# Attention scores from one stacked 128-row product and one 64-row product in two row tiles, with V's bias added later

## What is computed

```
xn   = group_norm(x, 32 groups) * w + b
qkv  = W_qkv @ xn + b_qkv              # 1536 x 512; 8 heads, 64 channels each for q, k, v
s    = (q^T k) / sqrt(64)              # per head, 1024 x 1024
p    = softmax(s over keys)
a    = p v^T                           # per head, 1024 x 64
out  = x + W_proj @ a + b_proj
```

## Time and profile before

| | |
|---|---|
| median of 3 runs | 4349.01 us (4347.39 to 4350.95) |
| span of the profiled execution | 4346.0 us |
| time around the span, to the median | 3.0 us |
| mean granted TensorE clock | 0.999 of full speed |
| busy share PE, DVE, ACT, POOL | 99, 76, 66, 58% |

### The profile page before, as it was taken

The page is one execution under the profiler, slowest core; times in us unless marked ns, Lnnn a source line. Parts: engine busy times, 40 slices in busy tenths (PEclk is TensorE's granted clock), DMA queues, the critical chain, the costliest instruction groups (busy, mean ns, idle before and its releaser), DMA issues.

```text
span 4346.0 us, 89905 instructions
## 1 busy us (share of the span) xinstructions
PE 4295.6 (99%) x26692; PEld 3736.9 (86%) x26692; DVE 3313.6 (76%) x5483; ACT 2875.3 (66%) x5317; POOL 2505.1 (58%) x2406
## 2 busy tenths in 40 slices
PE   7999999999999999999999999999999999999999
PEld 6888888888888888888888888888888888888887
DVE  5777867788687786777867778687786877868778
ACT  4757747477474775747757476574765747667476
POOL 5655556565564655656566565565655646556465
PEclk9999999999999999999999999999999999999999
DMA  3232222322223222222222222222222222223222
GB/s 87 48 96 47 71 72 48 96 47 80 64 46 96 49 78 64 56 86 49 80 71 66 81 46 80 65 66 79 48 79 64 71 71 49 79 64 82 60 49 92
DMA packets 99933, 295.61 MB, mean 68 GB/s; under 512 B 15136, under 2 KB 15264, under 8 KB 99616
## 3 DMA queue, kind: packets, MB, share of 16 engines
q1 hardware_dynamic: 99616, 291.71, 25.0%
HBM read 123.88 MB, written 33.55 MB: 36 GB/s over the span
## 4 chain that ended last, share of the span: by engine, by line
PE 95%; DVE 2%; issue 1%; POOL 1%; ACT 1%; DMA 0%; SPq 0%; DVEq 0%; ACTq 0%; POOLq 0%
PE ps_t L760 21%; PE ps_g L714 15%; PE ps_o L772 11%; PE ps_o L773 11%; PE ps_s L751 11%; PE ps_s L749 11%; PE ps_s L714 7%; PE ps_t L714 6%; PE ps_o L714 3%; POOL x_raw L389 1%; ACT probs L479 0%; DVE spread L603 0%; DVE pt_lo L569 0%; DVE work L601 0%; PE ps_t L778 0%
## 5 line engine op out<-in xcount | busy, mean ns | idle before, releaser
L383 POOL TENSOR_SCALAR probs<-probs,row_rcp 128x1024 f32<-128x1024 f32 x1024 | 1149.9, 1123 | 1375.5 <-DVE row_rcp L564 1374.0
L560 DVE TENSOR_REDUCE row_min<-ps_s 128x1 f32<-128x1024 f32 x1024 | 1250.2, 1221 | 220.5 <-PE ps_s L751 205.0
L484 ACT CAST pt_hi<-ps_t 128x512 fp32r<-128x512 f32 x2048 | 1110.6, 590 | 446.5 <-PE ps_t L760 431.7
L569 DVE TENSOR_TENSOR pt_lo<-ps_t,pt_hi 128x512 fp32r<-128x512 f32 x2048 | 1308.5, 679 | 9.5 <-ACT pt_hi L484 5.0
L479 ACT ACTIVATE probs<-ps_s,row_min 128x1024 f32<-128x1024 f32 x1024 | 1150.7, 1124 | 215.5 <-DVE row_min L560 202.5
L760 PEld LDWEIGHTS ps_t<-const_sb,probs 128*128 128x128 f32 x8192 | 944.3, 140 | 185.5 <-DVE pt_lo L569 57.0
L760 PE MATMUL ps_t<-const_sb,probs 128*128 128x128 f32 x8192 | 1085.9, 274 | 0.8
L772 PE MATMUL ps_o<-pt_hi,v_st 128*128 128x256 f32 x4096 | 1044.4, 288 | 0.0
L773 PE MATMUL ps_o<-pt_lo,v_st 128*128 128x256 f32 x4096 | 1014.8, 282 | 0.0
L751 PE MATMUL ps_s<-kl_st,q_st 128*128 128x512 f32 x2048 | 808.3, 395 | 0.0
L772 PEld LDWEIGHTS ps_o<-pt_hi,v_st 128*128 128x128 f32 x4096 | 771.6, 188 | 39.4 <-issue 12.4
(11 more groups left out here) (110 smaller groups left out, 4918.2 us busy)
## 6 DMA issues: line engine op xcount, KB each, us to landing
wqk_raw<-in_wqk SPq DMA_DIRECT2D x130, 256.0 KB, 2.7
q_st<-kh_st SPq DMA_DIRECT2D x128, 256.0 KB, 2.9
q_st<-kl_st SPq DMA_DIRECT2D x128, 256.0 KB, 3.6
kh_st<-kh_st SPq DMA_DIRECT2D x128, 256.0 KB, 2.9
kl_st<-kl_st SPq DMA_DIRECT2D x128, 256.0 KB, 3.5
x_raw<-layer_out SPq DMA_DIRECT2D x36, 512.0 KB, 5.0
wv_raw<-in_wv SPq DMA_DIRECT2D x68, 256.0 KB, 3.6
x_raw<-in_x SPq DMA_DIRECT2D x32, 512.0 KB, 5.3
```

Of the source, the lines that this page charges most:

```text
L383: nc.gpsimd.tensor_scalar(probs[m % 2][:, :], probs[m % 2][:, :], row_rcp[:, m % 4:m % 4 + 1], 1.0, ALU.mult, ALU.mult).then_inc(probs_rea ...
L484: nc.scalar.copy(pt_hi[:, m // 2 % 2, 4 * half:4 * half + 4, (m % 2) * P:(m % 2 + 1) * P], ps_t[:, half, :].rearrange("p (b t) -> p b t", ...
L560: nc.vector.tensor_reduce(row_min[:, m % 4:m % 4 + 1], ps_s[:, m % 2, :], AX.X, ALU.min).then_inc(min_ready, 1)
L569: nc.vector.tensor_tensor(pt_lo[place], ps_t[:, half, :].rearrange("p (b t) -> p b t", b=4), f32(pt_hi[place]), ALU.subtract).then_inc(lo_ ...
```

## The change

`scores` still has four matmuls of 512 columns per tile. The first two are the 128-row products of the stacked q (high over low) with the stacked high keys, one for each half of the keys. The other two contract 64 rows only, q high with k low. The one for the first 512 keys reads partitions 0 to 63 (`q_st` and `kl_st`), the one for the second 512 reads partitions 64 to 127 (a new tile `q2_st`, and `kl_st`); they write different PSUM banks. The product of the two low parts is no longer made.

`stack` gets a third copy before its inner wait (q high to the bottom of `q2_st`), and its last copy moves half as many columns.

V's bias leaves `evac_v`, which becomes a plain copy, and is added in `add_halves`, which becomes a three-operand instruction with the bias of the channel as a scalar. (The weights of a softmax row sum to one, so the bias passes through.) The broadcast `bv_all` gives way to a small `bv_sb`. The small statistics tiles become slices of one tile.

```diff
-        bv_all = sb("bv_all", [P, LAYERS, C], F32)
+        q2_st = [sb(f"q2_st{s}", [P, T], F32R) for s in range(2)]
+        bv_sb = sb("bv_sb", [P, LAYERS * KT], F32)
...
                 sp.dma_start(f32(q_st[s][0:D, :]), f32(kh_st[s][0:D, :])).then_inc(q_moved, 16)
                 sp.dma_start(f32(q_st[s][D:P, :]), f32(kl_st[s][0:D, :])).then_inc(q_moved, 16)
-                sp.wait_ge(q_moved, 32 * (hd + 1))
+                sp.dma_start(f32(q2_st[s][D:P, :]), f32(kh_st[s][0:D, :])).then_inc(q_moved, 16)
+                sp.wait_ge(q_moved, 48 * (hd + 1))
                 sp.dma_start(f32(kh_st[s][0:D, :]), f32(kh_st[s][D:P, :])).then_inc(stacked[s], 16)
-                sp.dma_start(f32(kl_st[s][0:D, :]), f32(kl_st[s][D:P, :])).then_inc(stacked[s], 16)
+                sp.dma_start(f32(kl_st[s][0:D, 0:HALF]), f32(kl_st[s][D:P, 0:HALF])).then_inc(stacked[s], 16)
...
-            sp.dma_start(bv_all[:, :, :], bv.rearrange("(o l) n -> o l n", o=1).broadcast_to([P, LAYERS, C])).then_inc(const_loaded, 16)
+            sp.dma_start(bv_sb[:, :], bv).then_inc(const_loaded, 16)
...
-                nc.vector.tensor_tensor(attn[rows, cols], ps_o[rows, 0:GROUP], o_part[k % 2][rows, :],
-                                        ALU.add).then_inc(attn_ready, 1)
+                nc.vector.scalar_tensor_tensor(out=attn[rows, cols], in0=ps_o[rows, 0:GROUP],
+                                               scalar=bv_sb[rows, bass.ds(lay * KT + p, 1)], in1=o_part[k % 2][rows, :],
+                                               op0=ALU.add, op1=ALU.add).then_inc(attn_ready, 1)
...
-                nc.vector.tensor_tensor(v_raw[:, b, :].rearrange("p (o n) -> p o n", o=1),
-                                        v_bank[b].rearrange("p (o n) -> p o n", o=1),
-                                        bv_all[:, bass.ds(lay, 1), :], ALU.add).then_inc(v_evac, 1)
+                nc.vector.tensor_copy(v_raw[:, b, :], v_bank[b]).then_inc(v_evac, 1)
...
-                j = m % NT
-                for half in range(2):
-                    cols = slice(half * HALF, (half + 1) * HALF)
-                    nc.tensor.matmul(ps_s[:, m % 2, cols], q_st[s][:, j * P:(j + 1) * P], kh_st[s][:, cols],
-                                     start=True, stop=False)
-                    mm = nc.tensor.matmul(ps_s[:, m % 2, cols], q_st[s][:, j * P:(j + 1) * P], kl_st[s][:, cols],
-                                          start=False, stop=True)
+                tile = slice((m % NT) * P, (m % NT + 1) * P)
+                top, low = slice(0, D), slice(D, P)
+                first, second = slice(0, HALF), slice(HALF, T)
+                for cols in (first, second):
+                    nc.tensor.matmul(ps_s[:, m % 2, cols], q_st[s][:, tile], kh_st[s][:, cols], start=True, stop=False)
+
+                nc.tensor.matmul(ps_s[:, m % 2, first], q_st[s][top, tile], kl_st[s][top, first], start=False, stop=True)
+                mm = nc.tensor.matmul(ps_s[:, m % 2, second], q2_st[s][low, tile], kl_st[s][low, second],
+                                      start=False, stop=True)
                 mm.then_inc(scores_ready, 1)
```

More of the change, by code:

```diff
@@ L119, in build @@
         bo_sb = sb("bo_sb", [P, LAYERS * KT], F32)
+        bv_sb = sb("bv_sb", [P, LAYERS * KT], F32)
         nw_sb = sb("nw_sb", [P, LAYERS * KT], F32)
         nb_sb = sb("nb_sb", [P, LAYERS * KT], F32)
[L122 to L125, removed]
+        row_stats = sb("row_stats", [P, 16], F32)
+        qk_scale = row_stats[:, 12:13]
+        row_min, row_sum, row_rcp = (row_stats[:, 4 * n:4 * n + 4] for n in range(3))
         bn_part = sb("bn_part", [P, KT, 12], F32)
@@ L570, in low_part, with add_halves @@
                                         f32(pt_hi[place]), ALU.subtract).then_inc(lo_ready, 1)
-            def add_halves(pair, k):
+            def add_halves(pair, lay, p, k):
                 rows = slice(0, D) if k < 4 else slice(D, P)
@@ L627, in x_low, with evac_v @@
                                         ALU.subtract).then_inc(xn_ready, 1)
-            def evac_v(i, lay, b):
+            def evac_v(i, b):
                 dve.wait_ge(v_acc, 8 * i + b + 1)
-                nc.vector.tensor_tensor(v_raw[:, b, :].rearrange("p (o n) -> p o n", o=1),
-                                        v_bank[b].rearrange("p (o n) -> p o n", o=1),
-                                        bv_all[:, bass.ds(lay, 1), :], ALU.add).then_inc(v_evac, 1)
+                nc.vector.tensor_copy(v_raw[:, b, :], v_bank[b]).then_inc(v_evac, 1)
             def output(i, lay, q):
@@ L662, in _, with pair_steps @@
                 x_low(0, c)
-            def pair_steps(i, p, last):
+            def pair_steps(i, lay, p, last):
                 pair = PAIRS * i + p
@@ L668, in pair_steps @@
                     if not last and m >= 4 and m % 2 == 0:
-                        add_halves(pair, m // 2 - 2)
+                        add_halves(pair, lay, p, m // 2 - 2)
                     if not (last and m + 2 >= PT_STEPS):
@@ L674, in pair_steps @@
                     if m == PT_STEPS - 1 or last and m >= 3 and m % 2 == 1:
-                        add_halves(pair, (m - 3) // 2)
+                        add_halves(pair, lay, p, (m - 3) // 2)
                     if not (last and m + 2 >= PT_STEPS):
@@ L685, in pair_steps @@
                     group_spread(i + 1)
-                add_halves(pair, 7)
+                add_halves(pair, lay, p, 7)
             with dve.Fori(0, PASSES) as i:
@@ L690, in _ @@
                 for b in range(4):
-                    evac_v(i, lay, b)
+                    evac_v(i, b)
                 for m in range(2):
                     smallest(TILES * i + m, m)
-                    evac_v(i, lay, 4 + 2 * m)
+                    evac_v(i, 4 + 2 * m)
                     reciprocal(TILES * i + m, m)
-                    evac_v(i, lay, 5 + 2 * m)
+                    evac_v(i, 5 + 2 * m)
                 with dve.Fori(0, PAIRS - 1) as p:
-                    pair_steps(i, p, False)
-                pair_steps(i, PAIRS - 1, True)
+                    pair_steps(i, lay, p, False)
+                pair_steps(i, lay, PAIRS - 1, True)
                 norm_coefs(i + 1, within(next_pass(i) // B, 0, LAYERS - 1))
@@ L921 @@
         "bqk": columns(qkv_b[:, :, 0:2].reshape(LAYERS, H * P)),
-        "bv": qkv_b[:, :, 2].reshape(LAYERS, C),
+        "bv": columns(qkv_b[:, :, 2].reshape(LAYERS, C)),
         "bo": columns(both("proj_b", "out_b")),
```

## The result

The changed kernel takes 4450.48 us (median of 4 runs, 4449.88 to 4450.77), the one before 4348.27 us (4 runs): a ratio of 1.0234, 95% interval 1.0219 to 1.0248. It is 102 us slower. The forecast was 4264 us and faster; the range, 4175 to 4505, holds the time, on its slow side. The rival "the passages drain the array" had forecast 4498.

A forecast was written before the change was run, and what follows sets the result against it. TensorE was taken as the bound, with DVE pacing some steps. Scores -89, bias +5 and start -1 gave -85 us against a span of 4346.0, so 4261, and 4264 us with the 3.0 around it; range 4175 to 4505.

The forecast's parts named there:

- the passages drain the array: Rival: each change between 128-row and 64-row products costs 0.16 us, one load exposed, -0.196 a tile, 4498 us; chance 0.25.
- the third price: In scores, the array's change from 128-row to 64-row products and back, twice per tile: taken as nothing, bounds 0 to 0.27 each.
- The second price: In scores, weight loads of the two 64-row matmuls: only one made ahead, so the second tile starts 0.109 us late.
- Drained, and loads only after it: Rival: each change of row count waits for the array to empty, then loads; -0.415 us a tile, 4721 us; chance 0.12.
- The first price: In scores, whether the two 64-row matmuls overlap: taken as yes, costing one matmul, 0.2325 us, and not two.
- Which tiles collect it: Tiles gaining the 0.124 us: 14 in each of three pairs, 1 in the last, 2 in the opening; 720 in all, 89 us.
- The cover that the rivals took: TensorE's waits for DVE, taken to absorb loss in the drain rivals: 0.4 us a pair, 2.3 in a pass's last pair.
- Stacking: Third copy ahead of the inner wait: a delay of 1 to 2 us in the opening, hidden; cost nothing.
- Bias: Three-operand add_halves takes 0.03 us more where DVE paces, 11 times in each of 16 passes: +5 us; evac_v nothing.
- The start: TensorE's first matmul waits until 12.10 us for bv_all; the small bias load lands 1 us earlier: -1 us.
- both loads hidden: Rival: both 64-row weight loads hidden and changes of row count free, saving 0.2325 us a tile, 4186 us; chance 0.20.
- the forecast's own sum: Scores per tile: 0.2325 saved less 0.109 for one exposed load, 0.124 us; lost from 0.062 us per change of row count.

The follow-up runs named there:

- e3: Changed kernel with both 64-row products on the same row tile (partitions 0 to 63), so not side by side: 4675.52 us, ratio 1.0756 to before.
- e1: Kernel before, its scores and stacking kept, with only V's bias moved into the addition of the halves: 4359.6 us against 4346.77, ratio 1.003.
- e8: Kernel before, with V's bias added by ACT in its copy of the other half and DVE's addition two-operand: 4383.08 us against 4353.95, ratio 1.0065.
- e2: Changed kernel with the two low products made as 128-row products; order, third copy and moved bias kept: 4361.39 us against 4346.77, ratio 1.0033.
- e5: Changed kernel with the 64-row pair ahead of the two 128-row score products: 4488.39 us against 4353.95, ratio 1.0307.
- e9: Changed kernel, timing only, with the 64-row pair made twice on even tiles and never on odd: 4320.93 us against before's 4347.16, ratio 0.9939.
- e4: Changed kernel with score matmuls ordered high, low, high, low, so four changes of row count per tile and no overlap: 5067.46 us, ratio 1.1658 to before.
- e7: Full-row version of the changed kernel with its two low products cut to 96 rows: 4367.12 us against before's 4353.95, ratio 1.0029.

## Why the prediction was wrong

**The step that failed is the third price**, "the passages at nothing, since the nearest row of a change of kind shows nothing". They cost 0.20 and 0.15 us, against bounds of 0 and 0.27. The row that I leaned on, scores to transposes without a gap, has both sides at 128 rows; it says that operands of another kind cost nothing, and can't say what other tiles cost. The Trainium skill, "TensorEngine Tiling (Array Packing)", Key Properties, has the rule that I set beside it: a change of tiling mode drains the engine. These traces agree with it in kind: no load and no matmul of the new mode starts until 0.32 us after the start of the last matmul of the old one. Here a passage costs 0.15 to 0.20 us: 0.09 of waiting, and 0.11 or, in front of the transposes, 0.06 for a load that isn't made early (e3).

**The second price, one load exposed (0.109), was wrong too**, and in the other direction: inside a mode the loads of the two tiles start together and none is exposed between them (2073.67 for both). The right sum per tile is 0.2325 - 0.20 - 0.15 = -0.12, where the forecast had +0.124 and the drain rival -0.196. Its 4498 us came near the measured 4450 in part by luck: it took 0.16 for the wait alone, where the starts show 0.09, had no load behind a passage, and charged one between the two tiles. In kind it is the heavier rival, "Drained, and loads only after it", that the traces bear out, a wait and then a load; its 0.27 a passage was too high, and so was the second load.

**The first price, overlap, was right**: both start at 2073.67. Its worth shows in e3: some 225 us. The sentence from the Trainium skill, "TensorE: Matmul & The Clock Gate", Part 3, that a further tile costs about 4 ns, agrees as far as the records, in steps of 0.01 us, can tell: in the timelines read the starts of a pair differ by 0.01 us at most.

**Which tiles collect it.** That 48 of 64 tiles of a pass stand at TensorE's pace and the last pair's mostly don't was right in kind: a pair of heads lost 1.75 us of the 1.88 that its passages cost, the last pair only some 0.5 of the 1.65 that 14 of its tiles would have cost. The cover that the rivals took for a pair, 0.4 us, was 0.13, and for the last pair 1.1 and not 2.3. I had called the last pair's pace DVE's; e1 and e8 show a ring of DVE and ACT.

**Stacking** at nothing: right, by e2 and by the wait of 0.9 us over the whole span.

**Bias** at 5 us: 13 alone (e1). The addition grew by 0.062 us and not 0.03, beyond the row on 512 columns, and it cost 0.28 a pair in the ordinary pairs, where I had 0.03, and nothing in the last, where I had 0.24. In the changed kernel it lies hidden in the ordinary pairs: 1.88 for the passages less 0.13 is all of the 1.75 us that a pair lost, and nothing is left for the bias. The changed kernel without the moved bias was not run. `evac_v`, where I allowed a shorter copy, stayed at 0.692 us.

**The start** gained 12.10 - 10.8 = 1.3 us, where I had 1.

Open is why the load costs 0.06 in front of the transposes and 0.11 in front of a long matmul; e3 and e5 show the sizes and not the cause. Open too is what the wait of 0.09 consists of. A kernel that shares a passage between two tiles and computes the reference wasn't built: the scores of the next tile wait for the exponential of two tiles back, because `ps_s` holds two tiles.

## What to carry to other kernels

Two 64-row products side by side cost one, but the way into 64-row tiles and back costs 0.35 us here, one and a half 512-column matmuls. Packing one pair between 128-row work lost 2.3% here, and two pairs in a row gained 0.6% (e9), where the second pair cost one matmul for two. More than two in a row wasn't run. Count products per passage, not products. A gap in the weight path in front of a matmul, with load and matmul starting together, is what such a passage looks like in a profile.

When no row shows an instruction's form, a row of a similar form isn't evidence of zero; where a cost from both sides decides the sign, the choice of zero has to be argued like any other. The middle of the bounds, 0.135 a passage, was on the slow side of the break-even of 0.116 that holds with both loads hidden, if only just, and well beyond the 0.062 of the forecast's own sum.

## What the runs showed of the hardware

- A change between 128-row and 64-row products cost 0.20 us ahead of a 512-column matmul, in both directions (e4, e5), and 0.15 ahead of 128-column transposes (1.02 us for 0.87). 96-row products among 128-row ones cost nothing that can be measured (e7).
- Between two passages, the loads of the two row tiles start together (2073.67), and a load on the same row tile starts while the matmul ahead still runs: in e3 at 1980.02, 0.23 us before its own matmul, which takes the usual 0.23; in e9 the second pair costs 0.23.
- The three-operand form of DVE on 64 x 256 takes 0.483 us for 0.421 with two; a plain copy of 128 x 512 out of PSUM takes what the addition took, 0.692. ACT's copy of 64 x 256 takes 0.366 us (e1), and with a bias 0.470 (e8).
